# Half tiles in the fifth round of a graph kernel's slots, stored and loaded as pair records, and the attribute loads of the last sums moved from SyncE to ScalarE

## The reference

```python
msgs = trans[edge_type, src]
agg = jax.ops.segment_sum(msgs, dst, num_segments=num_nodes)
...
msgs = norm[:, None] * x[col]
agg = jax.ops.segment_sum(msgs, row, num_segments=n)
...
rec_attr = _scatter_mean(edge_attr, row, N)
```

## Time and profile before

| | |
|---|---|
| runs without the profiler | 2645.38, 2645.51, 2649.59 us; median 2645.51 |
| profiled execution: span of its instructions | 2969.2 us (no other time of this execution is given) |
| TensorE busy in it | 2492.2 us, 84%, mean granted clock 0.913 |
| VectorE, ScalarE, GpSimd busy | 1808.3 (61%), 868.5 (29%), 1585.9 us (53%) |
| DMA | 520.11 MB, mean 175 GB/s |
| first loop | 104 to 745 us of the span |
| layer 1, tiles and windows | 806 to 962 and 962 to 1207 |
| layers 2 to 4 | 1352 to 1740, 1740 to 2130, 2130 to 2525 |
| last sums | 2781 to 2920 |

### The profile page before, as it was taken

One profiled execution on the slowest core, in us unless ns is written; L12 is line 12 of the kernel. 1 busy time (PEld: TensorE's weight loads), 2 busy tenths in 40 slices (PEclk: granted clock), 3 DMA queues, 4 the chain that ended last, 5 costly groups with the idle time before them and its releaser, 6 DMA issues.

```text
span 2969.2 us, 45704 instructions
## 1 busy us (share of the span) xinstructions
PE 2492.2 (84%) x15625; PEld 2211.7 (74%) x15625; DVE 1808.3 (61%) x6126; ACT 868.5 (29%) x1546; POOL 1585.9 (53%) x1706
## 2 busy tenths in 40 slices
PE   7587878888687899746999998998989897878798
PEld 3366666666387889436999997888988886777797
DVE  4565656575576777423876655676865554433585
ACT  2355555554354111213222231111311110443102
POOL 0656666663577666542566626666456665565200
PEclk9789888888799999857999999999999999898899
DMA  7312112110398666106888887877788774565793
GB/s 273 111 50 53 51 51 53 51 52 25 103 281 260 166 173 170 38 27 210 274 272 270 269 266 231 240 228 211 238 273 251 226 234 134 174 213 198 232 267 105
DMA packets 271515, 520.11 MB, mean 175 GB/s; under 512 B 61999, under 2 KB 115554, under 8 KB 270501
## 3 DMA queue, kind: packets, MB, share of 16 engines
q1 hardware_dynamic: 185053, 289.49, 31.2%
q0 software_dynamic: 86224, 227.59, 26.6%
HBM read 323.93 MB, written 192.99 MB: 174 GB/s over the span
## 4 chain that ended last, share of the span: by engine, by line
PE 69%; issue 10%; DMA 7%; DVE 6%; another core or an unknown queue 4%; ACT 2%; POOL 2%; SPq 0%; DVEq 0%; POOLq 0%; ACTq 0%
PE ps L1058 21%; PE ps L1030 10%; PE ps L892 7%; PE ps L1043 6%; PE ps L1245 5%; PE ps L1289 4%; PE ps L886 4%; PE ps L878 4%; DMA chunks<-xs 2%; DMA rec<-chunks,idx 2%; DMA srow<-lanes_of_slots 1%; DVE shot L2033 1%; POOL attributes L744 1%; PE ps L1112 1%
## 5 line engine op out<-in xcount | busy, mean ns | idle before, releaser
L735 POOL DMA_INDIRECT rec<-chunks,idx x596 | 588.5, 987 | 500.5 <-PE ps L1058 184.9
L1058 PE MATMUL ps<-dhot,rec 128*128 128x168 f32 x4768 | 757.2, 312 | 70.4 <-issue 35.3
L1058 PEld LDWEIGHTS ps<-dhot,rec 128*128 128x128 f32 x4768 | 703.8, 194 | 99.6 <-issue 77.6
L2054 DVE TENSOR_SCALAR dhot<-iota,dcode 128x168 f32<-128x168 f32 x2384 | 584.6, 311 | 216.7 <-remote 102.4
L1030 PE MATMUL ps<-hrow,shot 126*128 126x128 f32 x4000 | 516.3, 284 | 63.8 <-issue 29.5
L735 POOL DMA_INDIRECT msg<-messages,idx_buf x416 | 398.2, 957 | 307.3 <-issue 189.7
L1030 PEld LDWEIGHTS ps<-hrow,shot 126*128 126x128 f32 x4000 | 493.7, 199 | 81.7 <-issue 65.9
L1386 ACT ACTIVATE xs<-ps 128x512 f32<-128x512 f32 x500 | 295.1, 597 | 763.5 <-PE ps L1030 393.8
L744 POOL DMA_INDIRECT attributes<-w,rank_to x352 | 353.2, 1004 | 213.1 <-issue 102.2
L2033 DVE TENSOR_SCALAR shot<-srow,lane_no 126x512 f32<-126x512 uint8 x500 | 230.2, 486 | 117.4 <-PE ps L1030 51.2
L892 PE MATMUL ps<-big,lane1h 128*128 128x300 f32 x832 | 231.6, 432 | 9.3 <-issue 8.0
(11 more groups left out here) (304 smaller groups left out, 2538.6 us busy)
## 6 DMA issues: line engine op xcount, KB each, us to landing
chunks<-xs SPq DMA_DIRECT2D x375, 256.0 KB
tmp<-inverse_counts SPq DMA_DIRECT2D x36, 1008.0 KB
chunks<-xs SPq DMA_DIRECT2D x125, 258.0 KB
srow<-lanes_of_slots SPq DMA_DIRECT2D x100, 320.0 KB
grec<-chunks SPq DMA_DIRECT2D x125, 256.0 KB
messages<-big SPq DMA_DIRECT2D x25, 504.0 KB
trow<-lanes_of_targets SPq DMA_DIRECT2D x30, 320.0 KB
rec<-chunks,idx POOLq DMA_INDIRECT x596
```

The costliest lines, as they stand in the source:

```text
L735: eng.indirect_dma_start(buf, None, table, bass.IndirectOffsetOnAxis(ap=index, axis=0)).then_inc(sem, 16)
L1058: last = mm(ps[:, 4 + i % 2, (v % 3) * WT:(v % 3 + 1) * WT], rec[:, v % RS, j * P:(j + 1) * P], dhot[:, v % DS, j * WT:(j + 1) * WT], star ...
L2054: last = vec.tensor_scalar(dhot[:, v % DS, j * WT:(j + 1) * WT], iota[:, 0:WT], dcode[:, v, j:j + 1], None, ALU.is_equal)
```

## The change

The fifth round has tiles of 256 slots: 128 lanes of two. So a block has room for 2304 edges, and there are 450 columns of slots in place of 500. A record keeps four slots in 516 values, but as two *pairs* of 256 values and two codes each, so that a half tile, whose lane holds one pair, is stored by one transfer: two lanes make a record. In layers 2 to 4 a full tile is stored with all 516 columns. In the first loop VectorE works out lane and column of ranks from 2048 on in another way, in the last 12 groups. In the last sums one transfer loads a half tile's records: lane 2l takes a record from its start and lane 2l + 1 the same record from 32 values on, 480 values each, and the two slots of each lane stand first. The attribute loads are issued by ScalarE, with the copies of the mean attributes between them. The rest of the diff renames indices.

```diff
+FULL = NQ - TB
-NTILE = NQ * 4
+NTILE = 4 * FULL + 2 * TB
+LANE_ROWS = -(-NTILE // 4)
+HALF = P // 2
+BLOCK_RECS = (QS - 1) * P + HALF
-CAP = QS * SPAN
+CAP = 4 * BLOCK_RECS
-RECORD_COLS = 4 * P + 4
+PAIR = 2 * P + 2
+RECORD_COLS = 2 * PAIR
...
+        def slot_cols(n):
+            return 4 if n < FULL else 2
+        def first_col(n):
+            return 4 * n if n < FULL else 4 * FULL + 2 * (n - FULL)
+        def by_record(i):
+            return i % QS * TB + i // QS
+        def first_record(n):
+            return n % TB * BLOCK_RECS + n // TB * P
+        def pairs(row):
+            return row.rearrange("p (z c) -> p z c", z=2)
+        def rows_load(eng, i):
+            at, to = first_record(by_record(i)), grec[:, i % GR, :]
+            rows_ = x1_d[at:at + P, 0:4 * P]
+            if by_record(i) >= FULL:
+                to = to[:, 0:4 * P - 2 * A]
+                rows_ = bass.AP(rows_.tensor, rows_.offset, [[RECORD_COLS, HALF], [2 * A, 2], [1, 4 * P - 2 * A]])
+            else:
+                to = to[:, 0:4 * P]
+            eng.dma_start(to, rows_).then_inc(q(f"x1_stored_{i % GR}"), 16)
+        def attrs_load(eng, i):
+            at, cols = 4 * first_record(by_record(i)), slot_cols(by_record(i))
+            eng.dma_start(grec[:, i % GR, 4 * P:4 * P + cols * A],
+                          attr_d[at:at + cols * P, :].rearrange("(p j) a -> p (j a)", j=cols))\
+               .then_inc(q(f"x1_stored_{i % GR}"), 16)
...
-                    cols = RECORD_COLS if k == 1 else 4 * P
-                    at = (n % TB * QS + n // TB) * P
-                    eng.dma_start(x1_d[at:at + P, 0:cols], xs[:, i % XS, 0:cols])\
-                       .then_inc(q(f"x1_stored_{i % XS}"), 16)
+                    at = first_record(n)
+                    if n < FULL:
+                        eng.dma_start(x1_d[at:at + P, :], xs[:, i % XS, :]).then_inc(q(f"x1_stored_{i % XS}"), 16)
+                    else:
+                        eng.dma_start(x1_d[at:at + HALF, :].rearrange("l (z c) -> (l z) c", z=2), xs[:, i % XS, 0:PAIR])\
+                           .then_inc(q(f"x1_stored_{i % XS}"), 16)
-            eng.dma_start(srow_d.rearrange("(i c) p -> c i p", c=NQ), srow_u8[0:NQ]).then_inc(q("lanes_stored"), 16)
+            eng.dma_start(srow_d.rearrange("(i c) p -> c i p", c=LANE_ROWS), srow_u8[0:LANE_ROWS]).then_inc(q("lanes_stored"), 16)
-                eng.dma_start(grec[:, i % GR, 0:4 * P], x1_d[i * P:(i + 1) * P, 0:4 * P]).then_inc(q(f"x1_stored_{i % GR}"), 16)
-                eng.dma_start(grec[:, i % GR, 4 * P:], attr_d[i * 4 * P:(i + 1) * 4 * P, :].rearrange("(p j) a -> p (j a)", j=4))\
-                   .then_inc(q(f"x1_stored_{i % GR}"), 16)
+                rows_load(eng, i)
...
-                for j in range(4):
+                for j in range(slot_cols(tile_no(k, i))):
...
-                    act(xs[:, i % XS, 0:4 * P], ps[:, STAGE1_BANKS[i % 3], :], ACT.Copy).then_inc(q("x1_evac"), 1)
+                    z = slot_cols(tile_no(k, i)) // 2
+                    act(pairs(xs[:, i % XS, :])[:, 0:z, 0:2 * P], pairs(ps[:, STAGE1_BANKS[i % 3], :])[:, 0:z, :], ACT.Copy)\
+                        .then_inc(q("x1_evac"), 1)
+            attrs_sent(eng, 4)
+            for i in range(NQ):
+                if i >= GR:
+                    eng.wait_ge(q("gcn_sum"), i - GR + 1)
+                attrs_load(eng, i)
+                if i % (CB * QS) == 3 + GR and i > CB * QS:
+                    keep_means(i // (CB * QS) - 1)
...
+                    halves = g >= NEAR_STEPS[-1]
+                    if halves:
+                        st.did(vec.tensor_scalar(rank_i[:, 4, :], rank_i[:, 0, :], 1, P - 1, ALU.arith_shift_right,
+                                                 ALU.bitwise_and))
+                        st.did(vec.tensor_scalar(rank_i[:, 5, :], rank_i[:, 0, :], 2, None, ALU.bitwise_and))
+                        st.did(vec.tensor_scalar(in_half[:, 0, :], ranks_g, float(4 * P * (QS - 1)), None, ALU.is_ge))
                     st.settle()
-                    st.did(vec.tensor_copy(slot_lane[:, g % SUB, :], rank_i[:, 1, :]))
...
+                    if halves:
+                        st.did(vec.scalar_tensor_tensor(out=in_half[:, 1, :], in0=rank_i[:, 1, :], scalar=-1.0,
+                                                        in1=rank_i[:, 4, :], op0=ALU.mult, op1=ALU.add))
+                        st.did(vec.scalar_tensor_tensor(out=in_half[:, 2, :], in0=src_sb[:, g * G:(g + 1) * G], scalar=2.0,
+                                                        in1=rank_i[:, 5, :], op0=ALU.mult, op1=ALU.add))
+                        st.settle()
+                        st.did(vec.tensor_tensor(in_half[:, 1, :], in_half[:, 1, :], in_half[:, 0, :], ALU.mult))
+                        st.did(vec.tensor_tensor(in_half[:, 2, :], in_half[:, 2, :], in_half[:, 0, :], ALU.mult))
+                        st.settle()
+                        st.did(vec.tensor_tensor(slot_lane[:, g % SUB, :], in_half[:, 1, :], rank_i[:, 1, :], ALU.add))
+                        st.did(vec.tensor_tensor(rank_hi[:], rank_hi[:], in_half[:, 2, :], ALU.subtract))
+                    else:
+                        st.did(vec.tensor_copy(slot_lane[:, g % SUB, :], rank_i[:, 1, :]))
+                    st.settle()
...
-                    vec.tensor_scalar(shot[0:BS, i % SS, :], srow[0:BS, s_ % NS, (n % QS) * SPAN:(n % QS + 1) * SPAN],
+                    cols = slot_cols(n) * P
+                    vec.tensor_scalar(shot[0:BS, i % SS, 0:cols], srow[0:BS, s_ % NS, (n % QS) * cols:(n % QS + 1) * cols],
```

More of the change, by code:

```diff
@@ L1154, in _ @@
                     for j in range(4):
-                        last = mm(ps[0:NQ, 7, j * P:(j + 1) * P], src1[:, j * NQ:(j + 1) * NQ], wt("ident"), start=True,
-                                  stop=True)
+                        last = mm(ps[0:LANE_ROWS, 7, j * P:(j + 1) * P], src1[:, j * LANE_ROWS:(j + 1) * LANE_ROWS], wt("ident"),
+                                  start=True, stop=True)
                     last.then_inc(q("lanes_mm"), 1)
@@ L1286, in _ @@
                 record_got(eng, i)
-                for j in range(4):
+                cols = slot_cols(by_record(i))
+                for j in range(cols):
                     got = grec[:, i % GR, :].rearrange("p (m s a) -> p s m a", s=4, a=A)[:, j]
                     last = mm(ps[0:BS, 6 + b % 2, 0:P + A], ghot[:, i % GH, j, :], got, start=first_tile and j == 0,
-                              stop=last_tile and j == 3)
+                              stop=last_tile and j == cols - 1)
                 last.then_inc(q("gcn_sum"), 1)
@@ L2211, in slot_hots @@
                     eng.wait_ge(q("gcn_sum"), i - GH + 1)
-                for j in range(4):
-                    at = tile_slots(i) + j
+                for j in range(slot_cols(by_record(i))):
+                    at = first_col(by_record(i)) + j
                     last = vec.tensor_scalar(ghot[:, i % GH, j, :], iota[:, 0:BS], gcn_lo[:, at:at + 1], None, ALU.is_equal)
```

57 lines of the change are left out of this document (33 added, 24 removed).

## The result

The changed kernel has a median of 2627.75 us (7 runs, 2617.76 to 2638.6), the kernel before 2641.9 us beside it (7 runs). The ratio is 0.9946, with an interval of 0.9930 to 0.9962: faster by 14.3 us, with 10 to 18 inside the interval. The forecast was 2597.5 us, 48 us less, and its range ended at 2620. So the sign was right and the time lies outside the range. A second measurement of the same two kernels (run a0) gave 0.9950, 2621.37 against 2635.24 us.

The account below looks back on a forecast made before the run. TensorE was taken to bound most stages touched. Layers 2 to 4 -34.5, layer 1 -7, last sums -10, first loop +4, shorter table -0.5: -48 us from 2645.5, so 2597.5 us (chance 0.57), range 2579 to 2620.

Parts of the forecast that it names:

- Layers 3 and 4: Last rounds of 25 tiles, halved: 11 us less each, between 6 and 12.9, with GpSimd's floor 76.2 against 78.1 us.
- Rival (a): Whole kernel: the other engines, GpSimd and DMA, take most of the gain; -19 us, 2626 us; chance 0.20.
- The price of a tile: TensorE in layers 2 to 4: 1.03 us a tile, so halving 25 gives back 12.9 us a round.
- Layer 2: Last round of 25 tiles: TensorE full, GpSimd and VectorE below the new 63 us; 12.5 us less.
- The 516 columns: Full tiles' stores in layers 2 to 4: under 1% more bytes, covered by spare DMA share; cost 0.
- First loop: Last 12 of 52 groups: added VectorE operations and waits cost +4 us, between 0 and 10.6.
- Layer 1: Last 25 tiles: GpSimd becomes what ends last; 7 us less, between 2 and 13.
- The clock: TensorE's granted clock in layer 1's last round: stays up, at 1.00; a fall would cost layer 1 5 us.
- Last sums: Final stage: shorter blocks on TensorE, level with the transfers; 10 us less, between 3 and 13, near 129 us.
- the move of the loads: Last sums, attribute loads from SyncE to ScalarE: protects the gain, adds none except under half a us at the start.
- The store of lanes: Store before layer 1, outer dimension 125 to 113: covered, 0 us; at most 4 if GpSimd starts late.
- Rival (c): Last sums: half tiles' row loads run on one DMA engine, 14.8 us each; slower, 2840 us; chance 0.04.

Follow-up runs that it names:

- a_nosend: The changed kernel without 48 attribute stores of GpSimd in the fifth rounds of layers 3 and 4: 0.9857 of the kernel before.
- b0: The kernel before, unchanged, profiled a second time: 2648.65 us, span 2646.8 us.
- b_516: The kernel before, with layers 2 to 4 storing 516 columns in place of 512: 1.0022 of the kernel before.
- b_dve: The kernel before, with eight small unused VectorE operations and two more waits in each of the first loop's last 12 groups: 0.9999 of the kernel before.
- a_sp: The changed kernel, with the attribute loads of the last sums back on SyncE: 0.9948 of the kernel before.
- a_lanes128: The changed kernel, with 128 rows in the store of lanes in place of 113: 0.9928 of the kernel before.
- b_nosend: The kernel before without 48 attribute stores of GpSimd in the fifth rounds of layers 3 and 4: 0.9978 of the kernel before.

## Why the prediction was wrong, point by point

The two profiles are of one execution each, runs of one kernel scatter by 8 us and more, and the chips differ by some us. The terms below are therefore the better of a window and an interval, and they don't close to the microsecond.

- **Layers 3 and 4, forecast 11 us each: the step that failed.** The prediction held "a floor of 76.2 us, against 91 - 12.9 = 78.1", and "against it that GpSimd still waits 15 of 91 us". Both numbers were wrong. The 78.1 came from a long execution; the true starting point was 77.5 and 77.3 us, at GpSimd's floor already. And the floor left out the pauses that carry another name: the 62 transfers of the earlier trace rows at 1.28 us are 79.6 us, which is above 78.1 even in the rows that the prediction had. TensorE and GpSimd were both full before the change, so taking TensorE's work away was worth some 1 and 3 us. Rival (a), "the other engines take most of it", names what happened here. That its 2626 us is so near to 2627.75 is in part luck: it had 6 us for each of these rounds, since it too subtracted from 91, 3 for the last sums, which gave 10, and 8 lost in the first loop, which lost nothing.
- **The price of a tile**, "1.03 us a tile", was 16% too high. By the chain it is 0.89, and a half tile gives back 11.1 us a round.
- **Layer 2, forecast 12.5:** 74.0 to 67.7 and 66.6, so 6 to 7. The wrong price is 1.8 us of the miss. The prediction called GpSimd "below the new 63 us" from 49.53 + 11.0 = 60.5, by waits of which some were filed under other names; at 1.28 us each they are 63 to 64, level with it. That TensorE ends last there before the change was right, but the round stops some 4 us above TensorE's floor, and why is not shown: rounds of layers 3 and 4 with only 43 or 44 of GpSimd's operations still take 67.7 us (a_nosend).
- **The 516 columns, forecast 0:** about 5 us. The argument, "the cover is a DMA share of 0.75 to 0.90", was in its lower part read from the stretched rounds; in b0 the shares are 0.84 to 0.90. That added engine time shows in part while transfers run that close is my reading; b_516 shows only that it shows.
- **First loop, forecast +4:** 0, by b_dve. GpSimd paces the loop. The -0.5 us for the shorter table was not measured apart.
- **Layer 1, forecast 7:** 28.4 to 23.0 and 22.9, so 5.5. Right, inside 2 to 13. The clock did fall, to 0.85 from 0.94, while TensorE was busy 17 of 23 us, where the forecast was 1.00; the price of that is within the 5.5. GpSimd is busy 16.9 of 23.0 us, less than the "22.6" of the prediction, with 36 operations in place of the 41 counted (in b0 too: 19.07 us, 36). The chain of waits in this window shows two engines in turn:

```profile
792.46 6.64 DMA chunks<-xs
...
799.16 0.18 POOL xs L842
```

  Up to 799.1 us it runs through two stores of tiles, which the prediction had not expected to end last, and from there to the end through GpSimd's codes and attribute stores, as it had said.
- **Last sums, forecast 10 and "near 129":** 140.5 to 129.7 and 130.3. Right. A full block takes 5.52 us in b0 too, and one with the half tile 5.03 by a_sp's timeline (2505.77 to 2510.80). That the move of the loads only protects the gain also fits a_sp, as far as it can be told.
- **The store of lanes, forecast 0, at most 4:** right. GpSimd's late start came, 3.8 us, and by the time of layer 2 nothing of it can be told from the spread (a_lanes128). Rival (c), a load on one DMA engine, is excluded: last sums of 130 us leave no room for 25 loads of 14.8.

With the stores out of the way the account nearly closes. Forecast were 48 us and measured 32 between b_nosend and a_nosend. The windows of these two profiles give 8.2 for layer 2's fifth round (74.0 to 65.8), 6.7 and 8.8 for layers 3 and 4 (74.4 to 67.7, 76.5 to 67.7), 4.1 for layer 1 (26.7 to 22.6) and 8.0 for the last sums (139.3 to 131.3), 35.8 in all, less 5 for the stores' width: 31.

With the stores in place the windows sum to more than was measured: 6.5 + 4 + 5.5 + 10.5 for layer 2, layers 3 and 4 together, layer 1 and last sums, less 5 for the width, is 21.5 against 14.3. The sum is 7 us too large and 3 us outside the interval (10 to 18); I can't assign them.

The range failed mainly for one reason. Its end of 6 us a round in layers 3 and 4 was no bound, since a row that shows two engines full allows 0.

## What to carry to other kernels

Compare a profile's span with the median of unprofiled runs before costing anything from it; where they differ by 12%, the waits and the slack of that trace belong to that execution, and it should be profiled again or the slack bounded at nothing. Waits filed under "remote" in a program on one core were the sign of it in this trace. For an engine that issues one transfer after another, count operations times the distance from start to start, not busy time plus the waits that carry its name. And when a change lightens one of two full engines, look in the same stretch for work of the other that could be done elsewhere: here that was worth 17 to 20 us in the changed kernel, more than the change by itself, and 7 in the kernel before.

## What the runs showed of the hardware

- An indirect transfer of 128 rows costs GpSimd some 0.98 us and a further 0.30 us before the next one starts, the same for a gather of 2064-byte records and for a store of short attribute rows (a0 from 1740 us on). In the first loop the median from start to start is 1.25 us. In these stretches it is the number of transfers that counts. The Trainium skill (Perfetto Trace Analysis, DMA Instruction — SWDGE (GPSIMD)) says that the profile's end of such an operation is the end of writing descriptors and not of the transfer; equal durations for transfers of so different size, and landings of up to 8.50 us behind them, agree. Of the 0.30 us it says nothing.
- One store of 56.5 KB on SyncE with an outer dimension of 113 let the load behind it land 3.8 us later than one of 64 KB with 128 did (a0, a_lanes128).
- Two packets of 1024 bytes in place of one of 2064 cost 26 ns of a DMA engine for each packet more, and 26 us of the kernel's time at a DMA share of 0.91.
- Widening rows from 2048 to 2064 bytes in 375 stores raised the bytes of SyncE's queue by 0.3% (289.49 to 290.26 MB) and its engines' time by 2.5% (942 to 966 us). Why by so much was not tried.
- The same kernel had spans of 2969.2 and 2646.8 us in two profiled executions.
